# A gated attention and ffn stage: from two streams in a loop to halves of neighbouring groups, written out

## The reference

```python
# x: (2048, 256) residual stream, 32 sequences of 64 rows
x1 = x + o0 @ Wo0.T + bo0                     # end of the cross attention
ln = layernorm(x1)
q  = elu(ln @ Wq + bq) + 1;  k = elu(ln @ Wk + bk) + 1;  v = ln @ Wv + bv
kv = k.T @ v  (per sequence and head of 16)   # linear attention
x1 = x1 + (sigmoid(ln @ Wg + bg) * (q @ kv)) @ Wo + bo
ln = layernorm(x1)
h  = quantized(ln) @ ternary(w1).T            # 256 -> 1024, int8-like rows, weights -1, 0, 1
h  = silu(depthwise_conv1d(h, conv_w, conv_b))# three taps along the 64 rows of a sequence
x2 = x1 + quantized(h) @ ternary(w2).T        # 1024 -> 256
q3 = layernorm(x2) @ Wq3 / 4                  # queries of the next stage
```

## Time and profile before

| | before |
|---|---|
| median of 3 runs | 3893.89 us (3890.46 to 3898.93) |
| profiled execution, time | 3894.62 us |
| profiled execution, span | 3892.6 us |
| mean granted TensorE clock | 0.892 of 2.4 GHz |
| busy share of the span: TensorE, VectorE, ScalarE, GpSimd | 79%, 67%, 51%, 16% |
| the stage of the change, first instruction to the next stage's first | 1431.40 to 1933.44 us |
| in it, each of the four rounds | 115 us, 80 of them with VectorE busy |

### The profile page before, as it was taken

How to read it: one execution, slowest core, us unless ns; L and a number is a source line. 1 busy time by engine, 2 the same in 40 slices (tenths; PEclk the granted TensorE clock), 3 DMA queues, 4 the chain that set the end, 5 groups by cost and what they waited for, 6 DMA issues and landing times. The chain is left out here.

```text
span 3892.6 us, 99208 instructions
## 1 busy us (share of the span) xinstructions
PE 3063.7 (79%) x34478; PEld 2671.8 (69%) x34478; DVE 2590.2 (67%) x7538; ACT 1971.4 (51%) x4188; POOL 620.4 (16%) x741
## 2 busy tenths in 40 slices
PE   3449999999999964555379999999999999643574
PEld 3348888888888853443268888888888888532453
DVE  5558888888888836666666777776777777465001
ACT  1146766666666632223246666666666666421111
POOL 0223333333333210000121111111111111000101
PEclk7669999999999986777679999999999999865787
DMA  2123223233333220000111111111111111212511
GB/s 66 50 82 84 82 79 85 80 82 83 81 82 83 67 62 11 22 22 11 36 32 42 38 42 39 38 40 40 39 38 41 38 42 28 73 44 69 191 48 61
DMA packets 235433, 221.17 MB, mean 57 GB/s; under 512 B 69516, under 2 KB 228545, under 8 KB 234816
## 3 DMA queue, kind: packets, MB, share of 16 engines
q1 hardware_dynamic: 232896, 208.22, 18.9%
q0 software_dynamic: 2048, 6.68, 0.5%
HBM read 186.30 MB, written 28.39 MB: 55 GB/s over the span
## 5 line engine op out<-in xcount | busy, mean ns | idle before, releaser
L1892 DVE CUSTOM_DVE_ANT_0 xb_junk<-xb_ring,xb_mbias 128x372 bf16<-128x372 f32 (+2 forms) x1024 | 543.6, 573 | 177.6 <-PE xb_ring L1800 158.0
L1731 ACT ACTIVATE xb_P<-xb_sc 124x1024 f32<-124x1024 f32 (+1 forms) x416 | 426.0, 1026 | 374.5 <-PE xb_sc L1824 372.6
L879 PE MATMUL xa_acc<-xa_raw,xa_P 124*128 124x193 f32 x1664 | 315.6, 331 | 7.7 <-ACT xa_P L754 7.7
L1771 PE MATMUL xb_ring<-xb_xst,xb_whi 128*128 128x372 f32 (+2 forms) x768 | 262.4, 369 | 38.6 <-DVE xb_xst L1871 32.8
L1800 PE MATMUL xb_ring<-xb_khi,xb_qhi 64*128 64x372 f32 (+2 forms) x1024 | 269.8, 404 | 26.4 <-DVE xb_klo L1877 17.3
L1771 PE MATMUL xb_ring<-xb_whi,xb_xst 128*124 128x256 f32 (+1 forms) x1248 | 285.3, 291 | 2.9 <-DVE xb_maxes L1892 0.6
L1824 PE MATMUL xb_sc<-xb_qhi,xb_khi 64*124 64x256 f32 (+1 forms) x1664 | 282.4, 372 | 0.0
L879 PEld LDWEIGHTS xa_acc<-xa_raw,xa_P 124*128 124x128 f32 x1664 | 266.4, 189 | 19.1 <-ACT xa_P L754 12.1
L1877 DVE TENSOR_TENSOR xb_klo<-xb_ring,xb_khi 128x372 fp32r<-128x372 f32 (+2 forms) x256 | 138.8, 572 | 208.7 <-ACT xb_khi L1697 207.7
L865 PE MATMUL xa_sc<-xa_qblk,xa_kT 128*124 128x128 f32 x1664 | 238.6, 272 | 0.0
L1771 PEld LDWEIGHTS xb_ring<-xb_whi,xb_xst 128*124 128x124 f32 (+1 forms) x1248 | 215.8, 187 | 23.0 <-DVE xb_maxes L1892 15.6
(11 more groups left out here) (418 smaller groups left out, 8222.9 us busy)
## 6 DMA issues: line engine op xcount, KB each, us to landing
xa_raw<-in_ctx SPq DMA_DIRECT2D x64, 279.0 KB
ex_w<-in_W SPq DMA_DIRECT2D x16, 1024.0 KB, 8.8
xa_raw<-in_ctx SPq DMA_DIRECT2D x32, 372.0 KB
xa_xTr<-in_ctxT SPq DMA_DIRECT2D x64, 186.0 KB
xb_raw<-in_ctxT SPq DMA_DIRECT2D x64, 186.0 KB
xa_xTr<-in_ctxT SPq DMA_DIRECT2D x32, 248.0 KB
xb_raw<-in_ctxT SPq DMA_DIRECT2D x32, 248.0 KB
xa_mask<-in_mask SPq DMA_DIRECT2D x32, 200.1 KB, 5.2
```

Of the source, the lines that this page charges most:

```text
L879: i = nc.tensor.matmul(acc[:, o, :], w, raw[0:KEYS, t3, t, :], start=t == 0 and o == 0, stop=t == NKT - 1, skip_group_check=True)
L1731: nc.scalar.activation(P[0:w, pbuf(c, p), :], sc[(c + p) % 2][0:w, :], ACT.Exp).then_inc(sem("exped"), 1)
L1771: i = nc.tensor.matmul(out, l, r, start=k == 0, stop=k == 4)
L1892: v.tensor_tensor_reduce(out=junk[:, k, 0:w], in0=ring[f % 3][:, 0:w], in1=mbias[:, p, k0:k0 + w], scale=1.0, scalar=-3.0e38, op0=ALU.add, ...
```

## The change

**Order.** The two streams are gone, and the loop too. The work of a group is cut into two halves, `attention(g)` (to the quantized second norm) and `ffn(g)` (from the spreading of the scale to the queries of the next stage). Each `yield` now gives a moment, and a planner, `by_time`, merges all 16 halves by moment when the program is built: group g's attention begins at 32 g, its ffn at 32 g + 31.5, in units meant as microseconds. So `ffn(g)` and `attention(g+1)` lie mixed on each engine, in straight-line code. There is one set of buffers, with `x1`, `xq`, `diag`, `xs`, `os` and `q3` doubled, and eight PSUM banks: pA to pD for the attention, pE, pF, pH for the slices, pG for the rest.

**Work.** Five row biases are added by TensorE: one more product for each 128 rows (fp32r, two rows of ones against the bias split into a high and a low part), so 10 more products a group. ScalarE takes over the exponential's bias, the max(z, 0) (as Relu), and the copy of the values out of PSUM. The gate is a tanh of half the argument in place of a sigmoid; the factor of a half goes into the copy of `lT`. The first 1/sqrt is taken by GpSimd with the exponent -0.5, three times a group, so that no logarithm is left. The maximum over `h2` is taken in two halves of 1024 numbers, the first in the midst of the conv part. The loads are split in two, and the first group's attention begins when the first part is there; w1 and w2 are made ternary in the gaps of that attention.

The diff, cut to its core:

```diff
+def by_time(*works):
+    nexts = [(begin + next(work), k) for k, (begin, work) in enumerate(works)]
+    while nexts:
+        _, k = at = min(nexts)
+        nexts.remove(at)
+        begin, work = works[k]
+        t = next(work, None)
+        if t is not None:
+            nexts.append((begin + t, k))
...
+    EVERY, SECOND = 32, 31.5
...
+        def biased(out, xT, name, b):
+            for t in range(GROUP):
+                for k in range(2):
+                    nc.tensor.matmul(out[:, t, :], xT[:, k, TOK * t:TOK * t + TOK], wm[name][:, k, :], start=k == 0, stop=False)
+                i = nc.tensor.matmul(out[:, t, :], rowsr[:], bhl[:, BIASES.index(b)], start=False, stop=True)
+            return i
+        def groups(*parts):
+            works = []
+            for g in range(NG):
+                works += [(g * EVERY + begin, part(g)) for begin, part in zip((0, SECOND), parts)]
+            by_time(*works)
...
         @block.gpsimd
+            def rstd(b, tag, r):
+                pool.wait_ge(sem(tag + "_var"), r)
+                wait_apart(pool)
+                nc.gpsimd.tensor_tensor(b.rstd[:], b.var[:], mhalf[:], ALU.pow).then_inc(sem(tag + "_rstd"), 1)
...
         @block.scalar
-            with act.Fori(0, R) as r:
-                in_turn(work, streams, r)
+            def attention(g):
+                yield 7.5
+                act.wait_ge(sem("lT_ps"), 2 * g + 1)
+                nc.scalar.activation(lT[:], dim(pB), ACT.Copy).then_inc(sem("lT"), 1)
+                yield 11
+                act.wait_ge(sem("q_ps"), g + 1)
...
+                for o in range(2):
+                    nc.scalar.activation(qe[:, o], dim(pC)[:, o], ACT.Exp, bias=bq[:, o:o + 1])
+                act.wait_ge(sem("k_ps"), g + 1)
+                nc.scalar.activation(ke[:], tok(pD), ACT.Exp)
+                nc.scalar.activation(kb[:], tok(pD), ACT.Relu).then_inc(sem("ke"), 1)
+                for o in range(2):
+                    i = nc.scalar.activation(qp[:, o], dim(pC)[:, o], ACT.Relu, bias=bq[:, o:o + 1])
+                i.then_inc(sem("qe"), 1)
...
+                yield 14.5
+                act.wait_ge(sem("g_ps"), g + 1)
+                nc.scalar.activation(gb[:], tok(pB), ACT.Tanh, scale=0.5).then_inc(sem("gb"), 1)
...
         @block.tensor
+            def attention(g):
+                yield 0
+                pe.wait_ge(sem(f"x_in{g % 2}"), 32 * (g // 2 + 1))
+                pe.wait_ge(sem("gt"), g)
+                biased(tok(pA), os_[:, g % 2], "WoT0", "bo0").then_inc(sem("y_ps"), 1)
...
+            def ffn(g):
...
+                yield 0
+                pe.wait_ge(sem("diag"), g + 1)
+                pe.wait_ge(sem("hs"), g * NF)
+                for t in range(GROUP):
+                    i = nc.tensor.matmul(pH[:, TOK * t:TOK * t + TOK], ones[:], diag[:, g % 2, t, :], start=True, stop=True)
+                i.then_inc(sem("s_ps"), 1)
...
         @block.vector
-                b.chain.step(v.tensor_tensor(b.x1[:], tok(b.pA), b.xs[:], ALU.add))
-                b.chain.step(v.tensor_tensor(b.x1[:], b.x1[:], wide("bo0"), ALU.add))
-                yield from layer_norm_vector(nc, b.chain, b.sem, "a", b.nb, b.x1, b.ln, r)
+            def attention(g):
+                X = x1[:, g % 2]
+                yield 1.5
...
+                v.tensor_tensor(X, tok(pA), xs[:, g % 2], ALU.add).then_inc(sem("x1"), 1)
+                dve.wait_ge(sem("x1"), g + 1)
+                variance(nb, "a", X)
+                yield 4.5
...
+                normed(nb, "a", X, ln, 2 * g + 1)
...
+            def ffn(g):
...
+                for f in range(NF):
+                    yield 3.7 + 1.9 * f
...
+                    v.tensor_tensor(padded[:, f % 3, :, 1:S + 1], h_bank(f).rearrange("p (b s) -> p b s", s=S),
+                                    srow[:].rearrange("p (b s) -> p b s", s=S), ALU.mult).then_inc(sem("hs"), 1)
+                    yield 5.3 + 1.9 * f
+                    dve.wait_ge(sem("hs"), g * NF + f + 1)
+                    dve.wait_ge(sem("mid"), g * NF + f + 1)
...
+                    if f == 5:
+                        yield 5.5 + 1.9 * f
+                        dve.wait_ge(sem("h2"), g * NF + NF // 2)
+                        v.tensor_reduce(top[:, 0], h2[:, 0:NF // 2].rearrange("p f t -> p t f"), AX.X, ALU.max, apply_absolute_value=True)
```

655 lines of the change are left out of this document (354 added, 301 removed).

## The result

The median went from 3894.32 us (four runs, 3890.46 to 3898.93) to **3864.22 us** (four runs, 3859.16 to 3867.06): a ratio of 0.9921, 95% interval 0.9904 to 0.9938. The direction held, but of 52 us forecast 30 came. The time lies outside the forecast's own range (3826 to 3858) and inside the wide one (3808 to 3872), in the part of it that was drawn for the rivals C and D. The profiled execution took 3861.7 us, with a span of 3859.9 (before 3892.6). The stage now lasts from 1431.40 to 1899.78: 468.38 us in place of 502.04, 33.7 less; the rest of the program takes 1.0 more.

What follows compares the result with a forecast made beforehand. No engine was full; VectorE, the fullest, idled 35 us a round. VectorE's starts and waits summed to 50.2 us a group; with both ends the stage lost 52.4 us: 3842 us, own range 3826 to 3858, wide 3808 to 3872.

Steps and rivals of the forecast that it cites:

- C: Rival: GpSimd's power, exponential block, Wo's product and semaphores take longer, 2.9 us a group more: 3865 us; chance 0.15.
- D: Rival: after each table load ScalarE stands still another 1.28 us, 2.6 us a group: 3862 us; chance 0.03.
- The start: From the weights' mean at 1455.51, attention(0) runs alone for 27 us; first diagonal at 1482.5, first mixed group at 1487.5.
- Wo's product: Ahead of the add of the attention's output: product taken as 2.8 us, VectorE's wait 1.25, bounds 0.5 and 2.2.
- X: Start of VectorE's add to x1, from which the forecast counts all offsets in one mixed group.
- The cycle: One group, from one add to x1 to the next: 50.2 us, 36.6 work and 13.6 waiting, against 57.5 before.
- From the last X to the end: Last diagonal out at 1833.9, then ffn(7) alone for 43 us, another 3.9, stage end at 1881.
- TensorE keeps up: During slices 1 to 3: transposes, copy of lT, Wq and Wk end near X + 10.7.
- ScalarE's block: Exponential block ahead of slice 4's middle tap: 3.9 us, bounds 3.5 to 4.7, making VectorE wait 2.7 more.
- B: Rival: TensorE's clock stays at 1.00 through the gaps, 4.0 us a group less: 3810 us; chance 0.12.
- E: Rival: TensorE at 0.50 nearly always, its chain leads, 57 us a group: 3890, no visible change; chance 0.03.
- F: Rival, slower: GpSimd's power, three times a group, takes several microseconds; at 5.5 us the time is 3923; chance 0.04.

Runs made afterwards that it cites:

- the pair of runs: Changed kernel without ScalarE's table loads (3854.8 us), with 14 extra TensorE products ahead of Wq's product (3861.6), and with both together (3855.0).
- the run with extra work: Changed kernel plus 24 unused bf16 products on TensorE behind w2's products in each group: 3844.4 us, one run.
- The run in the old order: Kernel before, two streams kept, with row biases on TensorE and exponential, Relu and values copy on ScalarE: 3881.03 us, ratio 0.9962.

## Why the prediction was right, and where it was off

The gain was 52.4 us of stage by the sum, 33.7 in the trace, so 18.8 are missing there (by unrounded numbers); 1.0 more is in the rest of the program, and 2.5 is how far the median lies above the profiled execution. The miss is larger than the 16 us that the forecast's own range leaves; that the wide range holds it is owed to the prices of C and D, of which neither came about, and so is luck. The 18.8, piece by piece:

- **The start, 4.4.** The means of the weights come at 1456.10 (1455.51 forecast), but the second add of group 0 stands at 1480.34 where I had 1476.6, since Wo's product runs at half clock and VectorE waits 2.26 for it. X of the first mixed group is 1491.86, forecast 1487.5. The terms that I listed for this stretch add up to 25.8 us, not to the 27 that I used, so they fall short by 5.6.

```profile
1480.34 0.69 DVE L1458 TENSOR_TENSOR gf_x<-gf_pC,gf_x 128x512 f32<-128x512 f32 x1 [2.26 <-PE gf_pC L1119]
...
1491.86 0.69 DVE L1434 TENSOR_TENSOR gf_x<-gf_pA,gf_xs 128x512 f32<-128x512 f32 x1 [3.98 <-PE gf_pA L1119]
```

- **The cycle, 8.7 in six.** Forecast 50.2, measured 51.3 in five and 53.4 in the first. Along the list, forecast against measured offset from X: slice 1's copy 4.95 and 5.33 (the power, 0.51 of waiting for 0.3, within its bounds); end of slice 3 11.2 and 11.6; slice 4 15.9 and 16.2; first maximum 18.8 and 18.9; gate 25.2 and 25.2; h2 32.2 and 32.4; add behind Wo (32.2 + 1.06 + 1.25) 34.5 and 35.3; second norm 39.6 and 40.4; third norm's end 47.5 and 48.5; next X 50.2 and 51.3. The largest miss is **Wo's product**: taken 2.8 us with its bias passes and a wait of 1.25, by a clock that rises on the way. It rose too late: 3.41 us at a mean granted clock of 0.57, low until the last 0.6 us or so. The wait is 1.79 (1.5 to 2.0 in the other groups), inside its bounds of 0.5 and 2.2. In the first cycle slice 4 waits 2.81 for TensorE where the later ones wait 1.49, since the transposes ahead of Wq's product are at half clock already (1.12 us for four, 0.66 later) and Wk's begins there too; slice 2's taps wait 1.36 for ScalarE instead of 0.74.
- **From the last X to the end, 5.7.** "TensorE keeps up" failed in ffn(7), where no other work is mixed in. Wq3's product of ffn(6) stands ahead of slice 1 and takes 3.78 at half clock:

```profile
1852.13 3.78 PE L187 MATMUL gf_pG<-gf_lT,gf_Wq 128*128 128x256 f32 x8 [0.26 <-ACT gf_lT L1279]
```

VectorE waits 2.25 for slice 1. The first slice comes 4.6 us behind the diagonal, not 3.5. VectorE waits 0.94 for the norm's power and 1.13 for w2's tail, and ffn(7)'s own Wq3 takes 3.78 where I had 3.3.

So the mechanism stood: VectorE's chain with its waits sets the cycle. What was mis-sized, at each end and in the middle, is mostly the same term: fp32 products on a TensorE at half clock that I had at a full clock (Wq and Wk ahead of slice 4, Wq3 ahead of slice 1 in ffn(7)) or at a rising one (Wo). What came as forecast: 2.07 us a slice with 0.74 idle; 1.73 idle ahead of h2 (1.7); 2.80 ahead of x1's add at clock 0.50 (2.7).

**Slice 4 was right in size and wrong in its reason.** I had ScalarE's block alone with 2.7 more; it is 1.49 for TensorE and then 1.75 for ScalarE, 3.24 against 0.74 in a plain slice: 2.5 more. "TensorE keeps up: transposes, copy of lT, Wq, Wk end near X + 10.7" was the step that failed: slice 4's product starts at X + 12.7, behind Wq's 3.68 us. The block ends where I had it because both paths end there, as the pair of runs shows; that the size came out right is luck. Slice 5 came 3.7 behind slice 4, not 5.4, since slice 4's copy itself was late.

**The bias passes.** The estimate of 0.12 us each at full clock fits the 0.21 at half clock that the run without two of them shows. "They cost only where VectorE waits for the product they end" holds too.

**The rivals.** B (clock at 1.00) did not happen; the run with extra work shows 2.4 us at the last wait where B had 2.35. C is what the time looks like (3865), but not for its reasons: the power was 0.2 longer, not 0.6, the block not longer at all; only Wo's product came near C, with 0.54 us of its 0.95. D is out: the loads take 1.28 and the Silu starts 0.01 later. The rule of the Trainium skill that D rested on (ScalarE: Activation LUTs, What ACT_TABLE_LOAD costs), a drain of about 1.38 us with each switch, shows in no row here; its 1.28 us for the load itself are what the rows have. E is out: VectorE's chain leads. F is out: the power took 0.69 to 1.00 us.

**Where the gain comes from.** The prediction priced work and order as one shorter group, 50.2 for 57.5 us. The run in the old order takes this apart: 14.4 us of the 30 are there without any new order, and what the six cycles save beyond that (22.8 us) the two ends take back (23.2), so that the rest is the earlier first add. The sum had these terms, the early start and 43 us of ffn(7) alone among them, but not their balance.
